# A gate computed with tokens as rows, placed around the first attention scores, and two projected banks ahead of the second turned half

## The reference

```python
# 1: attention row sums through a tiny MLP
q, k = rope(ln(x) @ Wq.T), rope(ln(x) @ Wk.T)          # bf16 after the projection
o = where(causal, exp(q @ k.T / 16), 0).sum(-1)        # (4, 1024, 1)
x = x + ln(relu(o @ fc1_w.T + fc1_b) @ fc2_w.T + fc2_b)
# 2: mixture of experts, 8 experts, the best 2 for each token
flat = ln(x).reshape(4096, 256)
logits = flat @ gate_w + gate_b                        # (4096, 8)
topv, topi = top_k(logits, 2); topw = softmax(topv)
final = sum over experts e of routing[:, e] * (gelu(flat @ w1[e] + b1[e]) @ w2[e] + b2[e])
x = x + ln(final)
```

## Time and profile before

| | |
|---|---|
| median of 3 runs | 636.8 us |
| profiled execution, its own time | 638.7 us |
| span of the profiled execution | 636.9 us |
| PE busy | 545.6 us, 86% |
| DVE busy | 424.5 us, 67% |
| ACT busy | 365.3 us, 57% |
| POOL busy | 187.3 us, 29% |
| mean granted PE clock | 0.936 of full speed |

### The profile page before, as it was taken

How to read it: one execution, slowest core, us unless ns; L and a number is a source line. 1 busy time by engine, 2 the same in 40 slices (tenths; PEclk the granted TensorE clock), 3 DMA queues, 4 the chain that set the end, 5 groups by cost and what they waited for, 6 DMA issues and landing times.

```text
span 636.9 us, 14628 instructions
## 1 busy us (share of the span) xinstructions
PE 545.6 (86%) x4170; PEld 500.3 (79%) x4175; DVE 424.5 (67%) x1444; ACT 365.3 (57%) x836; POOL 187.3 (29%) x153
## 2 busy tenths in 40 slices
PE   1968788686896989999999999999999999999940
PEld 1737365462775989999999989989998999998940
DVE  5799698996887665545555557487388655455477
ACT  3455766684570746364554665685688563553582
POOL 2000045244535653242322412312312232421320
PEclk9968969798797999999999999999999999999985
DMA  8930011362215833232232353384374232322479
GB/s 216 361 118 1 1 67 67 114 236 87 90 43 185 237 87 60 50 44 39 52 48 50 45 161 63 58 247 91 46 246 88 51 50 50 44 39 50 99 186 326
DMA packets 51853, 66.79 MB, mean 105 GB/s; under 512 B 4870, under 2 KB 45292, under 8 KB 51692
## 3 DMA queue, kind: packets, MB, share of 16 engines
q1 hardware_dynamic: 37804, 47.87, 23.9%
q0 software_dynamic: 14016, 18.56, 16.9%
HBM read 38.26 MB, written 28.74 MB: 105 GB/s over the span
## 4 chain that ended last, share of the span: by engine, by line
PE 68%; DVE 16%; issue 5%; ACT 4%; DMA 4%; POOL 1%; DVEq 1%; SPq 0%; POOLq 0%; ACTq 0%
PE pY L1635 28%; PE pL L1623 24%; PE pP L759 6%; DMA sum_y<-y,dest 3%; PE pP L861 2%; PE pS L776 2%; PE pX L455 2%; DVE z L1775 2%; DVE mstats L1003 2%; PE pT L744 1%; ACT probs L657 1%; PE pS L818 1%; ACT xrows L631 1%; POOL sum_y L533 1%; DMA x_all<-x 1%
## 5 line engine op out<-in xcount | busy, mean ns | idle before, releaser
L1558 ACT ACTIVATE h<-pL,b_now 128x256 f32<-128x256 f32 x272 | 112.3, 463 | 151.7 <-PE pL L1623 146.7
L533 POOL DMA_INDIRECT sum_y<-y,dest x68 | 110.2, 1621 | 269.4 <-DVE y L1679 256.9
L1635 PE MATMUL pY<-w_hi,h_lo 128*128 128x256 f32 x544 | 154.0, 283 | 3.5 <-DVE h_lo L1652 3.4
L1623 PE MATMUL pL<-xeT_hi,w_lo 128*128 128x256 f32 x544 | 151.4, 278 | 6.2 <-issue 6.1
L1652 DVE TENSOR_TENSOR h_lo<-h,h_hi 128x512 fp32r<-128x512 f32 x136 | 92.7, 691 | 91.7 <-ACT h_hi L1564 90.9
L1635 PE MATMUL pY<-w_hi,h_hi 128*128 128x256 f32 x544 | 150.7, 277 | 0.6 <-issue 0.6
L1623 PE MATMUL pL<-xeT_lo,w_hi 128*128 128x256 f32 x544 | 150.7, 277 | 0.0
L1635 PE MATMUL pY<-w_lo,h_hi 128*128 128x256 f32 x544 | 150.6, 277 | 0.0
L1623 PE MATMUL pL<-xeT_hi,w_hi 128*128 128x256 f32 x544 | 150.6, 277 | 0.0
L1623 PEld LDWEIGHTS pL<-xeT_hi,w_lo 128*128 128x128 f32 x544 | 102.0, 188 | 7.6 <-issue 7.6
L1635 PEld LDWEIGHTS pY<-w_hi,h_lo 128*128 128x128 f32 x544 | 102.2, 188 | 5.1 <-DVE h_lo L1652 4.6
(11 more groups left out here) (292 smaller groups left out, 847.5 us busy)
## 6 DMA issues: line engine op xcount, KB each, us to landing
w_stage<-w SPq DMA_DIRECT2D x16, 1024.0 KB
xt<-sorted_x SPq DMA_DIRECT2D x38, 260.0 KB
sum_y<-fill SPq DMA_DIRECT2D x1, 4352.0 KB, 19.9
w_stage<-sum_y SPq DMA_DIRECT2D x8, 512.0 KB, 8.0
out<-z SPq DMA_DIRECT2D x8, 512.0 KB, 5.9
x_all<-x SPq DMA_DIRECT2D x3, 1024.0 KB, 8.3
sorted_x<-fill SPq DMA_DIRECT2D x8, 260.0 KB
sum_y<-y,dest POOLq DMA_INDIRECT x68, 3.7
```

What stands on the lines that cost most here:

```text
L533: pool.indirect_dma_start(out=sum_y, out_offset=bass.IndirectOffsetOnAxis(ap=to[:, i:i + 1], axis=0), in_=rows[:, i, :], in_offset=None, c ...
L1558: a = act.activation(h[:, c, :], pL[:, bk, i * TM:(i + 1) * TM], ACT.Gelu, bias=b1_now[par][:, c:c + 1])
L1623: mm = pe.matmul(pL[:, bk, i * TM:(i + 1) * TM], w[:, 0, col], x[:, k, :], start=(k == 0 and w is lo), stop=(k == KC - 1 and x is xeT_lo))
L1635: mm = pe.matmul(pY[:, i, 0:D], s[:, c, rows], w[:, 1, c * D:(c + 1) * D], start=(c == 0 and s is h_lo), stop=(c == FC - 1 and w is lo))
```

## The change

The logits are computed with tokens as rows. For each tile of 128 tokens and each half of the 256 features the turned residual rows `x3T` (128x128) are the stationary side and the gate's weights (128x8) the moving side, so 16 products with 8 columns take the place of 4 with 512. The result lies in `pP`, needs no turning back and no copy by ACT; DVE adds the bias, now spread over all partitions, in one instruction at the start of `choose`, which then reads SBUF.

In PE's order the first half of the gate goes ahead of the first four scores, the second half between scores 3 and 4. Two of the eight banks are projected ahead of pieces 2 and 3 of the turning. For this ACT copies piece 0 after five normalised tiles and piece 1 after six, and pieces 2 and 3 behind the copy of bank 1; DVE takes low parts 0 and 1 ahead of the aggregate, and 2 and 3 behind the adds.

```diff
-            gateb = sa("gateb", [NE, 1], F32)
+            sa("pad_gateb", [P, 1], F32)
-            logitsT = sa("logitsT", [NE, 2, 512], F32)
+            gate_bias = sa("gate_bias", [P, 512], F32)[:, 0:NE]
+            logits = sa("logits", [P, 512], F32)[:, 0:TB * NE]
-            pLogT = pP[0:NE]
-            pLog = pT[:, 0, 0:TB * NE]
+            pLog = pP[:, 0, 0:TB * NE]
-                             (gateb[:], gate_b.rearrange("(e o) -> e o", o=1)),
+                             (gate_bias, gate_b.rearrange("(o e) -> o e", o=1).to_broadcast([P, NE])),
...
# ACT, take_qk
+                    if b > 0 and n == 1:
+                        turn_hi(b, range(2, 4))
...
-            def take_logits(c):
-                act.wait_ge(logits_done, c)
-                for h in range(2):
-                    act.wait_ge(logitsT_done, c * 2 + h + 1)
-                    act.activation(logitsT[:, h, :], pLogT[:, h, :], ACT.Identity,
-                                   bias=gateb[:, 0:1]).then_inc(logitsT_ready, 1)
...
                 take_hid(j)
-                norm_x(j + 1)
-                turn_hi(j + 1)
+                norm_x(j + 1, range(5))
+                turn_hi(j + 1, range(1))
+                norm_x(j + 1, range(5, 6))
+                turn_hi(j + 1, range(1, 2))
+                norm_x(j + 1, range(6, TB))
                 take_qk(j + 1, j + 1, split_from)
                 take_x3T(j)
-                sum_exps(j + 1, range(TB // 2))
-                take_logits(j)
-                sum_exps(j + 1, range(TB // 2, TB))
+                sum_exps(j + 1, range(TB))
                 weigh(j)
...
# PE
             def gate_half(c, h):
                 for k in range(KC):
                     pe.wait_ge(x3T_ready, c * 4 + KC * h + k + 1)
-                    mm = pe.matmul(pLogT[:, h, :], gatew[:, k, :], x3T[:, k, h * 512:(h + 1) * 512],
-                                   start=(k == 0), stop=(k == KC - 1))
-                mm.then_inc(logitsT_done, 1)
-
-            def turn_logits(c):
-                for t in range(TB):
-                    if t % 4 == 0:
-                        pe.wait_ge(logitsT_ready, c * 2 + t // 4 + 1)
-                    mm = pe.transpose(pLog[:, t * NE:(t + 1) * NE], logitsT[:, t // 4, t % 4 * P:(t % 4 + 1) * P],
-                                      ident[0:NE, 0:NE])
+                for t in range(h * TB // 2, (h + 1) * TB // 2):
+                    for k in range(KC):
+                        mm = pe.matmul(pLog[:, t * NE:(t + 1) * NE], x3T[:, k, t * P:(t + 1) * P], gatew[:, k, :],
+                                       start=(k == 0), stop=(k == KC - 1))
                 mm.then_inc(logits_done, 1)
...
                 attention_mlp(j)
-                turn_x(j + 1)
-                project(j + 1, j)
+                turn_x(j + 1, range(2))
+                project(j + 1, j, range(2))
+                turn_x(j + 1, range(2, 4))
+                project(j + 1, j, range(2, 8))
                 turn_x3(j, 0)
                 turn_x3(j, 1)
-                score(j + 1, range(TB // 2))
                 pe.wait_ge(qk_ready, (j + 2) * 8)
                 gate_half(j, 0)
+                score(j + 1, range(TB // 2))
                 gate_half(j, 1)
-                score(j + 1, range(TB // 2, 6))
-                turn_logits(j)
-                score(j + 1, range(6, TB))
+                score(j + 1, range(TB // 2, TB))
                 rank(j)
...
             gate_half(B - 1, 0)
             gate_half(B - 1, 1)
-            turn_logits(B - 1)
...
# DVE, mid
                 rsqrt(ch, mrstd[:, 0, :], mmv[:, :, 1], work)
-                if not last:
-                    between()
                 for t in range(TB):
...
+                if not last:
+                    between()
                 dve.wait_ge(attn_added, (c + 1) * TB)
...
# DVE, choose
-                dve.wait_ge(logits_done, c + 1)
+                dve.wait_ge(logits_done, 2 * (c + 1))
+                dve.tensor_tensor(logits.rearrange("p (t e) -> p t e", e=NE), pLog.rearrange("p (t e) -> p t e", e=NE),
+                                  gate_bias.rearrange("p (o e) -> p o e", o=1).to_broadcast([P, TB, NE]),
+                                  ALU.add).then_inc(logits_ready, 1)
+                dve.wait_ge(logits_ready, c + 1)
                 for t in range(TB):
-                    s = dve.max(top8[:, t, :], pLog[:, t * NE:(t + 1) * NE])
+                    s = dve.max(top8[:, t, :], logits[:, t * NE:(t + 1) * NE])
...
                 stats_attn(j)
+                turn_lo(j + 1, range(0, 2))
                 aggregate_attn(j)
-                turn_lo(j + 1, range(0, 2))
                 mid(j, lambda: turn_lo(j + 1, range(2, 4)))
```

More of the change, by code:

```diff
@@ L397, in build @@
         x3T_ready = sem("x3T_ready")
-        logitsT_done = sem("logitsT_done")
-        logitsT_ready = sem("logitsT_ready")
         logits_done = sem("logits_done")
+        logits_ready = sem("logits_ready")
         route_link = sem("route_link")
@@ L582, in _, with norm_x @@
             act.sem_inc(gexp_ready, ONE)
-            def norm_x(b):
+            def norm_x(b, tiles):
                 act.wait_ge(xn_stats, b + 1)
                 act.wait_ge(xn_turned, b * 4)
-                for t in range(TB):
+                for t in tiles:
                     act.activation(xn[:, t, :], x_all[:, b * TB + t, :], ACT.Identity,
@@ L590, in norm_x, with turn_hi @@
                                    scale=rstd[:, b * TB + t:b * TB + t + 1]).then_inc(xn_ready, 1)
-            def turn_hi(b):
+            def turn_hi(b, pieces):
                 act.wait_ge(projected, b * 8)
-                for n in range(2 * KC):
+                for n in pieces:
                     h, k = n // KC, n % KC
@@ L689, in weigh @@
                 act.activation(gexp[:], gdiff[:], ACT.Exp).then_inc(gexp_ready, 1)
-            norm_x(0)
-            turn_hi(0)
+            norm_x(0, range(TB))
+            turn_hi(0, range(4))
             take_qk(0, 0)
@@ L725, in _ @@
                 high_piece(act, 0, 0, 1, q)
-            take_logits(B - 1)
             act.activation(warm[:, 1:2], iota_e[:, 0:1], ACT.Exp)
@@ L734, in _, with turn_x @@
             pe.sem_inc(l2_done, ONE)
-            def turn_x(b):
-                for n in range(2 * KC):
+            def turn_x(b, pieces):
+                for n in pieces:
                     h, k = n // KC, n % KC
@@ L745, in turn_x, with project @@
                     mm.then_inc(xn_turned, 1)
-            def project(b, routed):
+            def project(b, routed, banks):
                 pe.wait_ge(ranks_read, routed + ONE)
-                for n in range(8):
+                for n in banks:
                     h, i, m = n // 4, (n // 2) % 2, n % 2
@@ L880, in _ @@
             pe.wait_ge(ident_in, 16)
-            turn_x(0)
+            turn_x(0, range(4))
             pe.wait_ge(set_up, 2)
-            project(0, 0)
+            project(0, 0, range(8))
             pe.wait_ge(tables_in, 64)
@@ L1097, in choose @@
                 ch = routing[c]
-                dve.wait_ge(logits_done, c + 1)
+                dve.wait_ge(logits_done, 2 * (c + 1))
[3 more added lines that the diff above has]
+                dve.wait_ge(logits_ready, c + 1)
                 for t in range(TB):
-                    s = dve.max(top8[:, t, :], pLog[:, t * NE:(t + 1) * NE])
+                    s = dve.max(top8[:, t, :], logits[:, t * NE:(t + 1) * NE])
                 ch(s)
                 for t in range(TB):
-                    s = dve.max_index(idx8[:, t, :], top8[:, t, :], pLog[:, t * NE:(t + 1) * NE])
+                    s = dve.max_index(idx8[:, t, :], top8[:, t, :], logits[:, t * NE:(t + 1) * NE])
                 ch(s)
```

## The result

The changed kernel took 647.76 us (median of 4 runs, 644.45 to 648.24) against 636.32 us for the kernel before on the same chip (4 runs, 634.84 to 636.99): ratio 1.0155, 95% interval 1.0128 to 1.0182. That is slower by 1.6%, and outside the predicted range. The profiled execution took 647.8 us with a span of 646.0 (before 638.7 and 636.9); its mean granted clock is 0.914 (before 0.936).

What follows compares the result with a forecast made beforehand. The prediction took a chain mostly through TensorE as the bound, with all edits before the expert loop. Two batches at 0.31 us plus 0.89 in the tail gave 1.5 us, so 635.3 us from 636.8; range 632.5 to 640.0.

Steps and rivals of the forecast that it cites:

- clock as before: Batches and tail: the granted clock was assumed unchanged by the new gate, so the sum holds no cost for a fall.
- The sum of 1.5 us: Whole kernel: 0.31 us gained in each of batches 0 and 1, plus 0.89 in the tail.
- rival C: Batch 0 or 1: clock falls, half a gate and the scores cost 3.7 us in that batch; chance 0.17.
- Twice gives 642.7: Batches 0 and 1: the clock falling in both gives 642.7 us in all; once gives 639.0.
- the tail's 0.9 us: Last sequence, gate to first top-8: 3.85 us instead of 4.74, so 0.89 us won.
- The pace of the loads: Gate on PE: each of 32 weight loads with its tiny product takes 0.109 us, 3.49 us in all.
- Rivals A, B and D: Gate load pace: A 0.115 to 0.135 us, chance 0.29; B 0.074 to 0.09 or earlier clock, 0.14; D over 0.138, 0.09.
- The gains: Batches 0 and 1: each becomes 0.31 us shorter through gate, projections and removed transposes.
- the 0.07 us of the earlier projections: Turning and projecting: PE starts at 85.95 us instead of 86.02, a gain of 0.07 us.
- The going of the transposes: Between scores 5 and 6: the 8 logit transposes of 0.59 us go, returning 0.20 us to the chain.
- Rival B's earlier clock: Start of projecting: full projections instead of transposes could raise the clock up to 2 us earlier; rival B's chance 0.14.
- Batch 2: Third batch: its own gain, 1.5 us or more on DVE, is swallowed by PE's wait for a fetched tile.

Runs made afterwards that it cites:

- the first experiment: The changed kernel's new gate in its new places, with turning and projecting ordered as in the kernel before: 649.04 us, ratio 1.0118 to the kernel before.

## Why the prediction was wrong

**The step that failed** is the term that the sum put at nothing: "clock as before". The sum of 1.5 us has no cost for a fall, and the case in which the clock falls among the loads (rival C) was given 0.17 on the ground that "gap, transposes and small scores passed without a fall" before. That evidence said nothing of the new element, 16 loads in a row with 8 columns behind each. Before, products with 512 columns stood there. With the 8-column loads the clock fell in two batches of the profiled execution, and these cost 9.0 us. The range left out two falls, though rival C had priced them at 642.7. The first sequence, where the scores had run at 1.2 GHz, was read, and was put down to the little work ahead of it.

**The size of C** was too small. Priced at half a gate and the scores, 3.7 us, it cost 4.87 and 4.15 us. Against the batch with 64 columns, from the gate's start to the hidden layer (15.72 against 10.28 us), the first half cost 0.91, the first four scores 0.83, the second half 1.53 and the rest of the scores 2.17 us, in all 5.44: the fall came in the first half of the gate and not in the second, so the term left out half of the gate and the four small scores. "Twice gives 642.7" became 647.8; a part of that gap is the tail's 0.9 us, which was counted as a gain and came out as a loss of 0.3.

**The pace of the loads** was right. Where the clock held, 32 took 3.49 us in the tail, 0.109 us each, the value taken. That it fits to the last digit is partly luck: it was the pace of a transpose, chosen as lying between the two ends. The rule cited beside it (the Trainium skill, TensorE: Matmul & The Clock Gate, section LDWEIGHTS: 107 ns for 128 columns) agrees, 0.107 us against 0.109, and the 0.074 us of the logits' transposes was indeed no measure for a true product. Rivals A, B and D fall by this, as far as they rest on the pace.

**The gains** are seen in part, and only in profiles, one of each kernel. Batches 0 and 1 with 64 columns are 0.29 and 0.60 us shorter than before, with 56 columns 0.40 and 0.05; 0.31 each was forecast. But the three kernels that changed the tail alone took 36.22 to 36.68 and 36.62 to 37.06 us for the same batches with unchanged code, so a gain of this size is hardly told from the scatter. Of its terms, the 0.07 us of the earlier projections is seen in batch 1 (7.81 us after the hidden layer against 7.88) and not in batch 0 (7.94 in both), and with 56 and 64 columns they start later in batch 1 (8.17 and 8.16). The going of the transposes was priced too low where it shows: from score 4 to the hidden layer are 4.8 us in three of the four batches with 56 or 64 columns, against 5.19 and 5.27 before, 0.4 to 0.5 us where 0.20 was counted; the fourth took 5.75, which stays unexplained.

**The tail's** gate to top-8 took 3.77 us for a forecast of 3.85, and in the changed kernel the stretch ahead of the gate lost more than that won. The clock of that stretch tells the profiles apart: with 6.8 us at 1.2 GHz there (the changed kernel and those with 32 and 64 columns) it took 24.25 to 24.59 us, with 3.4 us (the ten others) 23.17 to 23.48. That is how the 64-column kernel's top-8 comes at 185.11, as before (185.23), though its gate won 0.93 us. What decides between 3.4 and 6.8 is open.

**Rival B's earlier clock** isn't shown. From the start of turning or projecting to granted clock 1.00 are 2.8 to 6.2 us in the batches with the new order and 3.3 to 6.1 in those with the old one. The 5.6 us that the prediction started from and the 4.3 in the changed kernel's batch 1 both lie inside that scatter.

**Batch 2** kept nothing that can be seen, as forecast: DVE waited 2.55 us for the tile there. The batch took 41.68 us in the changed kernel and 42.52 and 42.60 with 56 and 64 columns, against 41.77 to 42.78 with the old gate.

**The whole** of 1.5 us is shown by no run: the two versions of the whole change without a fall in a batch gave 0.9993 and 1.0011, each interval some 0.2% to either side. The forecast 0.9976 is just inside one of them (64 columns, from 0.9975). The times from top-8 to the end, 451.3 to 459.4 us with the same code, bury the rest.

**Open** stays why the clock held in some batches with 8 columns (batch 2 of the changed kernel, batch 1 of the first experiment). They have the same instructions in the same order; what differs is when the batch lies in time. No run moved a batch in time alone, and no rule is offered.

## What to carry to other kernels

A series of weight loads with few moving columns can have TensorE busy all the time and still lose the clock; what stands behind it pays too, so price such a change by the stage up to the clock's return, not by the loads. Here two forms kept it: 8 columns stationary and 512 moving (no fall in 18 batches), and the 8 moving columns repeated to 56 or 64 (none in 6), which costs 0.04 to 0.05 us for a half of the gate (1.73 against 1.69 us for 16 loads). When a trace says that a stretch survived, ask whether it held the instruction that is new.

## What the runs showed that was not expected

- The granted clock fell from 1.00 to 0.50 with PE and PEld busy 1.00, within the first 16 loads of 128 columns with 8 moving ones, and stayed there for 13.6 us of nearly unbroken work (67.8 to 81.4, 108.7 to 122.4).
- At 1.2 GHz such a load takes 0.208 us, at 2.4 GHz 0.109: the load itself runs by that clock.
- 64 moving columns cost hardly more than 8 behind a load of 128: 16 loads with their products 1.73 to 1.79 us against 1.69 to 1.74.
- One kernel gave 1.0038 [1.0016, 1.0061] in one session and 1.0005 [0.9977, 1.0032] in another, 12 runs each: the first alone would have been read as a loss, and the two together show neither loss nor gain.
- With 8 moving columns the fall can also come behind the loads, among dense products: in the changed kernel's tail 0.4 us behind the last load.
